# Graph kernel on one Trainium2 core: the node stage moved into the convolution's loop, two node tiles beside every three edge groups

## The reference

```
y0, y1 = x0 @ lin1_w0, x1 @ lin1_w1          # per node, times node_vec1 / 8
w      = silu(edge_scalars @ fc_w1 / sqrt(8)) * 1.679 @ fc_w2 / 8   # per edge
mids   = products of w, y[src] and edge_attr # per edge, 512 wide
agg    = segment_sum(mids, dst) / sqrt(20)   # per node
o      = agg @ lin2 / sqrt(128)              # per node, times node_vec1
x1     = layernorm(x + sin(pi/8) * (x @ sc_w) + cos(pi/8) * o)
xp     = x1 @ lin_w ; a_i, a_j = xp * att    # what the attention layer gathers
```

## Time and profile before

| | |
|---|---|
| median of three runs | 4669.1 us (4668.15 to 4671.51) |
| profiled execution, own time | 4665.0 us |
| its span in the trace | 4663.6 us |
| PE busy | 4158.5 us (89%) |
| DVE busy | 3623.9 us (78%) |
| POOL busy | 3212.8 us (69%) |
| ACT busy | 1445.1 us (31%) |
| convolution's loop | about 81 to 2197 us |
| node stage | about 2197 to 2508 us |
| attention | 2514 us to the end |

### The profile page before, as it was taken

How to read it: one execution, slowest core, us unless ns; L and a number is a source line. 1 busy time by engine, 2 the same in 40 slices (tenths; PEclk the granted TensorE clock), 3 DMA queues, 4 the chain that set the end, 5 groups by cost and what they waited for, 6 DMA issues and landing times. The chain is left out here.

```text
span 4663.6 us, 115274 instructions
## 1 busy us (share of the span) xinstructions
PE 4158.5 (89%) x33992; PEld 2693.8 (58%) x33992; DVE 3623.9 (78%) x10643; ACT 1445.1 (31%) x3213; POOL 3212.8 (69%) x3384
## 2 busy tenths in 40 slices
PE   6988888888888888887997899999988999899997
PEld 5444444444444444443996666777666776666675
DVE  3777777777777777775775888888888888888887
ACT  4111111111111111111553344444444444444444
POOL 3777777777777777775003777777777777777774
PEclk8999999999999999999997888788888788888888
DMA  7444444444444444445774444444444444444443
GB/s 267 133 131 132 131 132 131 132 131 131 131 132 132 131 132 131 132 131 138 281 297 166 122 124 125 123 123 125 122 124 124 124 124 122 125 123 123 125 122 88
DMA packets 375419, 649.80 MB, mean 139 GB/s; under 512 B 130024, under 2 KB 249914, under 8 KB 373548
## 3 DMA queue, kind: packets, MB, share of 16 engines
q0 software_dynamic: 161120, 444.76, 34.6%
q1 hardware_dynamic: 214220, 204.13, 13.5%
HBM read 546.90 MB, written 101.68 MB: 139 GB/s over the span
## 5 line engine op out<-in xcount | busy, mean ns | idle before, releaser
L1995 POOL DMA_INDIRECT ord_xg<-xpa_rows,ord_meta x1666 | 1596.5, 958 | 510.9 <-issue 472.9
L869 POOL DMA_INDIRECT sub_xg<-y_rows,sub_meta x1668 | 1595.3, 956 | 510.5 <-issue 462.8
L2063 PE MATMUL ord_a<-ord_xg,ord_sel 128*128 128x264 f32 x3332 | 1144.5, 478 | 115.4 <-DVE ord_xg L2426 115.2
L919 PE MATMUL sub_a<-sub_mids,sub_sel 128*32 128x128 f32 (+1 forms) x13344 | 998.5, 305 | 228.8 <-DVE sub_mids L1081 221.2
L2063 PEld LDWEIGHTS ord_a<-ord_xg,ord_sel 128*128 128x128 f32 x3332 | 723.0, 238 | 254.3 <-DVE ord_xg L2426 122.9
L1081 DVE TENSOR_TENSOR sub_mids<-sub_w,sub_xg 128x384 f32<-128x384 f32 x1668 | 844.2, 548 | 0.0
L919 PEld LDWEIGHTS sub_a<-sub_mids,sub_sel 128*32 128x32 f32 x13344 | 438.1, 109 | 692.3 <-DVE sub_mids L1081 586.3
L1076 DVE TENSOR_TENSOR sub_mids<-sub_w,sub_xg 128x256 f32<-128x256 f32 x834 | 354.3, 425 | 522.0 <-DMA sub_xg<-y_rows,sub_meta 373.3
L989 ACT ACTIVATE sub_agg_s<-sub_a 128x256 f32<-128x256 f32 x556 | 213.9, 385 | 1618.6 <-PE sub_a L936 1543.3
L899 PE MATMUL sub_w<-sub_fc,sub_ht 64*128 64x256 f32 x3336 | 586.7, 429 | 0.0
L2426 DVE TENSOR_TENSOR ord_xg<-ord_xg,ord_prob 128x1024 f32<-128x1024 f32 x476 | 510.3, 1072 | 0.0
(11 more groups left out here) (183 smaller groups left out, 4153.4 us busy)
## 6 DMA issues: line engine op xcount, KB each, us to landing
sub_sum_rows<-sub_agg_s SPq DMA_DIRECT2D x556, 64.0 KB
mid_rows<-sub_sum_rows SPq DMA_DIRECT2D x14, 2240.0 KB, 8.7
sub_xg<-y_rows,sub_meta POOLq DMA_INDIRECT x1668
ord_xg<-xpa_rows,ord_meta POOLq DMA_INDIRECT x1666
ord_x_rows<-x_rows SPq DMA_DIRECT2D x119, 128.0 KB, 2.2
out_dram<-ord_res SPq DMA_DIRECT2D x119, 128.0 KB
xpa_rows<-mid_proj SPq DMA_DIRECT2D x14, 924.0 KB, 5.3
lin_xt<-in_x_t_dram SPq DMA_DIRECT2D x14, 896.0 KB, 9.9
```

The source lines that it names most:

```text
L869: nc.gpsimd.indirect_dma_start(xg[:, b, k], None, y, bass.IndirectOffsetOnAxis(ids[:, b, 0, k:k + 1], 0))\
L919: mm = nc.tensor.matmul(a[ROWS * m:ROWS * (m + 1), 0:w].rearrange("p (q f) -> p q f", f=MUL), sel[:, b, k, m], of, start=(j == 0), stop=False,
L1995: nc.gpsimd.indirect_dma_start(xg[:, b, k], None, xpa, bass.IndirectOffsetOnAxis(ids[:, b, k:k + 1], 0))\
L2063: mm = nc.tensor.matmul(psum_a[b % 2][:, 0:WIDE], sel[:, b, k], xg[:, b, k], start=(k == 0), stop=(k == TILES - 1 and not has(i, b, -1)), ...
```

## The change

`end_convolution` is no longer called on this path. A pair of node tiles (256 nodes) is worked on beside the three groups of a turn, in turns 1 to 45 (`with_pair`, `LOOP_PAIRS`). Pair i - 1 belongs to turn i. The four pairs that are left (`TAIL_PAIRS`) follow the loop in a short pipeline of their own. A pair may be done in turn i because all groups before turn i have then been summed and the nodes are sorted; the fit test of the inputs got a row for that (`late`). PE's node steps use the PSUM bank of `hidden` (`psum_h`) in turns with it, and stand ahead of the `weigh` of their pair of tiles. `hidden` moves from ahead of `add_up` of u = 1 and 3 to behind `weigh` of u = 0 and 1. Six more DMAs stand in SP's list in a turn. The diff, cut to its core:

```diff
+TURN_SUBS = SUB_TURN * GROUP_SUBS
+SUB_TURNS = math.ceil(SUB_GROUPS / SUB_TURN)
+NODE_PAIR = 2 * P
+NODE_PAIRS = NODES_PAD // NODE_PAIR
+LOOP_PAIRS = SUB_TURNS - 2
+TAIL_PAIRS = NODE_PAIRS - LOOP_PAIRS
...
+                def load_x(n, buf, past):
+
+                    if past is not None:
+                        wait_alone(sp, z_done, past)
+                        wait_alone(sp, pre_done, past)
+                    sp.dma_start(node_xt[:, buf].rearrange("p c j n -> p c (j n)"),
+                                 pair_xt_dram[:, :, bass.ds(n * NODE_PAIR, NODE_PAIR)]).then_inc(x_in[buf], 16)
+                    sp.dma_start(node_x[:, buf].rearrange("p j f -> p (j f)"), pair_rows(io["x"], n))\
+                        .then_inc(x_in[buf], 16)
...
+                def load_sums(n, buf, subs, past):
+
+                    if past is not None:
+                        wait_alone(sp, turned, 2 * past)
+                    wait_alone(sp, stored, stored_subs(subs))
+                    sp.dma_start(node_rows[:, buf].rearrange("p j q f -> p (j q f)"), pair_rows(sums, n))\
+                        .then_inc(sums_in[buf], 16)
...
+                def store_pair(n, buf):
+
+                    wait_alone(sp, out_done, n + 1)
+                    sp.dma_start(pair_rows(x1, n), out[:, buf].rearrange("p j f -> p (j f)")).then_inc(x1_out[buf], 16)
+                    wait_alone(sp, p_copied, 2 * n + 2)
+                    sp.dma_start(pair_rows(xpa, n), proj[:, buf].rearrange("p j f -> p (j f)"))\
+                        .then_inc(proj_out[buf], 16)
+                    sp.dma_start(pair_rows(att, n), proj_a[:, buf].rearrange("p j f -> p (j f)"))\
+                        .then_inc(proj_out[buf], 16)
...
@@ -841,12 +921,30 @@
                             load(g, b, i)
                         if is_pair(i, 0) and b == 0:
                             weights()
+                        if b == SUB_TURN - 1 and with_pair(i):
+                            load_x(i - 1, 0, None if is_pair(i, 1) else i - 1)
+                        if b == 0 and is_pair(i, SUB_TURNS - 1):
+                            for n, buf, times, _, _ in tail:
+                                load_x(n, buf, LOOP_PAIRS if times > 1 else None)
                         if has(i, b, -SUB_TURN):
                             store(g - SUB_TURN, b)
-                    if type(i) is int and i > 0:
+                    if with_pair(i):
+                        load_sums(i - 1, 0, TURN_SUBS * i, None if is_pair(i, 1) else i - 1)
+                        if not is_pair(i, 1):
+                            store_pair(i - 2, 0)
...
+                    if is_pair(i, SUB_TURNS - 1):
+                        for n, buf, _, _, _ in tail[0:-1]:
+                            load_sums(n, buf, TURN_SUBS * i, None)
+                        store_pair(LOOP_PAIRS - 1, 0)
                         for g in range(SUB_TURN * i, SUB_GROUPS):
                             store(g, g % SUB_TURN)
-                        sp.wait_ge(stored, stored_subs(SUBS))
+                        load_sums(tail[-1][0], tail[-1][1], SUBS, LOOP_PAIRS)
...
+                def bank_of_hidden(i, b, u, g):
+
+                    if (b, u) == (0, 4):
+                        pe.wait_ge(silu_done, 2 * g + 4)
+                        turn_sums(i - 1, 0, 0, psum_h)
+                    if (b, u) == (0, 5):
+                        pe.wait_ge(turned_copied, 2 * i - 1)
+                        turn_sums(i - 1, 1, 0, psum_h)
+                    if (b, u) == (1, 2):
+                        pe.wait_ge(silu_done, 2 * g + 4)
+                        add_self(i - 1, 0, i, psum_h)
+                    if (b, u) == (2, 2):
+                        pe.wait_ge(silu_done, 2 * g + 4)
+                        turn_normed(i - 1, 0, psum_h)
+                    if (b, u) == (2, 3):
+                        project(i - 1, 0, psum_h)
+                    if (b, u) == (2, 4):
+                        pe.wait_ge(p_copied, 2 * i - 1)
+                        project(i - 1, 1, psum_h)
...
-                            if u in (1, 3) and more:
-                                hidden(g + 1, after, after_i, u // 2, False)
                             for k in (2 * u, 2 * u + 1):
                                 add_up(g, b, i, k)
                                 if k % RUN == RUN - 1:
                                     hand_on(g, b, i, k // RUN)
+                            if with_pair(i):
+                                bank_of_hidden(i, b, u, g)
                             if u + 2 < PAIRS:
                                 weigh(g, b, u + 2, False)
                             elif more:
                                 weigh(g + 1, after, u + 2 - PAIRS, False)
+                            if u < 2 and more:
+                                if u == 0:
+                                    free_hidden(i, b)
+                                hidden(g + 1, after, after_i, u, False)
...
-                        for s in range(GROUP_SUBS):
-                            if s in (1, 2) and has(i, b, 1):
-                                silu(g + 1, (b + 1) % SUB_TURN, s - 1, not has(i, b, 1 - SUB_TURN))
-                            copy_out(g, b, i, s)
+                        more, early = has(i, b, 1), not has(i, b, 1 - SUB_TURN)
+                        if more:
+                            silu(g + 1, (b + 1) % SUB_TURN, 0, early)
+                        copy_out(g, b, i, 0)
+                        if more:
+                            silu(g + 1, (b + 1) % SUB_TURN, 1, early)
+                        copy_out(g, b, i, 1)
+                        if b == 2 and with_pair(i):
+                            take_normed(i - 1, psum_h, first)
+                            take_projected(i - 1, 0, 0, past, psum_h)
+                        copy_out(g, b, i, 2)
+                        if b == 0 and with_pair(i):
+                            take_sums(i - 1, 0, psum_h, first)
+                        if b == 2 and with_pair(i):
+                            take_projected(i - 1, 1, 0, past, psum_h)
+                        copy_out(g, b, i, 3)
+                        if b == 0 and with_pair(i):
+                            take_sums(i - 1, 1, psum_h, first)
+                        if b == 1 and with_pair(i):
+                            root(i - 1)
...
+                def fold(n, j, buf, times, first):
+
+                    dve.wait_ge(sums_in[buf], 16 * times)
+                    if not first:
+                        dve.wait_ge(turned, 2 * n + j - 1)
+                    f, rows = fold_rows[:, j], node_rows[:, buf, j]
+                    nc.vector.tensor_reduce(f[:, 0:MUL], rows[:, 1:4, 0:MUL].rearrange("p q f -> p f q"), AX, ALU.add)
+                    nc.vector.tensor_copy(f[:, MUL:].rearrange("p (q f) -> p q f", f=MUL), rows[:, 1:4, MUL:])\
+                        .then_inc(folded, 1)
+
...
+                def with_products(i, b, u):
+
+                    if (b, u) == (0, 4):
+                        fold(i - 1, 0, 0, i, is_pair(i, 1))
+                        fold(i - 1, 1, 0, i, is_pair(i, 1))
+                    if (b, u) == (1, 4):
+                        add_x(i - 1, 0, i, psum_h, is_pair(i, 1))
+                    if (b, u) == (1, 5):
+                        moments(i - 1)
+                    if (b, u) == (2, 1):
+                        normalise(i - 1, 0, None if is_pair(i, 1) else i - 1, is_pair(i, 1))
...
-                convolve_in_order(nc, io, c, y, sub_sums, kept)
-                end_convolution(nc, io, c, sub_sums, x1, xpa, att, 5, kept)
+                convolve_in_order(nc, io, c, y, sub_sums, x1, xpa, att, kept)
```

More of the change, by code:

```diff
@@ new lines, in turn_normed, with project @@
+                def turn_normed(n, buf, bank):
+                    pe.wait_ge(out_done, n + 1)
+                    for j in range(2):
+                        for h in range(2):
+                            mm = nc.tensor.transpose(bank[:, (2 * j + h) * P:(2 * j + h + 1) * P],
+                                                     out[:, buf, j, h * P:(h + 1) * P], c["ident"][:])
+                    mm.then_inc(t_done, 1)
+                def project(n, j, bank):
+                    pe.wait_ge(t_copied, n + 1)
+                    for h in range(2):
+                        mm = nc.tensor.matmul(bank[:, 0:FEAT + 2 * HEADS], out_t[:, j, h], c["w_proj"][:, h],
+                                              start=(h == 0), stop=(h == 1), skip_group_check=True)
+                    mm.then_inc(p_done, 1)
@@ L944, in turn, with free_hidden @@
+                def free_hidden(i, b):
+                    if b == 0 and with_pair(i) and not is_pair(i, 1):
+                        pe.wait_ge(p_copied, 2 * i - 2)
+                    if b == 1 and with_pair(i):
+                        pe.wait_ge(turned_copied, 2 * i)
+                    if b == 2 and with_pair(i):
+                        pe.wait_ge(pre_done, i)
                 def turn(i):
@@ new lines, in add_x @@
```

(48 more changed lines are left out.)

157 lines of the change are left out of this document (144 added, 13 removed).

## The result

The changed kernel takes **4819.8 us** (median of 4 runs, 4812.06 to 4826.46) against 4668.6 us (4667.36 to 4671.51) of the kernel before, measured beside it: ratio 1.0322, interval 1.0304 to 1.034. It is 151 us slower. The forecast was 4718 us, 50 us slower than before. The direction was right and the time lies inside the range given (4550 to 4840 us), but the loss is three times the one forecast. The profiled execution took 4819.5 us with a span of 4818.1.

A forecast was written before the change was run, and what follows sets the result against it. POOL's gathers were taken to set the pace, SP's list nearly as full. Removing 316.7 us and adding a 48 us tail gives 4396; 45 turns growing 7.05 us give 4713, put at 4718 us against the median; range 4550 to 4840.

The forecast's parts named there:

- The saving: Between the loop's last copy and the attention's first DMA: 316.7 us go, except for a tail.
- The late sums: At DVE's fold: sums land 23.1 us after SP's load, so DVE and PE stand still 5 us a turn.
- SP's list alone: SP's DMA list in a turn: 43.95 us as before plus six more DMAs, 50.1 us without contention.
- the 1 to 3 us put on top for delayed landings: SP's queue: the pair's 1.7 MB of transfers delay the landings of stores, 1 to 3 us a turn.
- the 51 to 53 us of that paragraph: Length of a turn by SP's list: 50.1 us plus 1 to 3 us for delayed landings.
- the 52.5 us of the next one: Length of a turn by the fold's wait: 38 - 8.6 + 23.1 us, ends 49.5 and 56.
- PE and DVE in a turn: Their work in the loop with the node steps added: 46.3 to 49 us a turn, 47 taken.
- some 2 us: Of PE's 40.5 us of earlier work a turn, this much was called modelled ends of matmuls.
- costs nothing more: PE's node steps ahead of `weigh` in the loop add no time where DVE still has a pair to multiply.
- from the fold to the end of group 3i + 2 PE needs 38 us: PE's stretch in the loop after the fold: 47 - 9.7 us and some slack.
- rival B: In the loop PE's standstill lowers its clock, 2 to 4 us more a turn, 4804 to 4916 us; chance 0.12.
- The tail: Four pairs left after the loop, up to the attention's first DMA: 48 us, bounds 35 and 60.

The follow-up runs named there:

- experiment 1: Changed kernel without the node stage's arithmetic, its six transfers a pair kept in SP's list; a turn takes 49.5 us.
- Experiment 4: Changed kernel with the fold of the sums two pairs later, transposes and products moved behind it; 4646.6 us, ratio 0.9938 to the kernel before.
- experiment 2: Changed kernel with the node arithmetic kept but no loads of sums or x in the loop after the first pair, and no stores; a turn takes 48.9 us.
- experiments 3 and 8: 3: changed kernel with PE's node step behind `weigh`, 4837.1 us; 8: same, plus fold two pairs later and x loads and stores on ScalarE's queue, 4680.1 us.
- Experiment 5: Changed kernel with twenty useless identity transposes on PE ahead of its wait for the fold, fold still late; 4756.0 us, ratio 1.0194 to the kernel before.
- experiments 11 and 12: A hundred useless PE transposes before the tail's sums: 11 on the twenty-transpose kernel, 4759.8 us; 12 on the steps-later kernel with ScalarE's queue, 4597.3 us.
- experiments 9 and 10: 9: changed kernel with a pair's steps one group later, 4682.3 us; 10: the same with x loads and stores on ScalarE's queue, 4593.0 us.

## Why the prediction was right in direction and wrong in size

**The saving** was right: the stage of 316.7 us is gone and the attention behind it is unchanged.

**The late sums** were right, in their place and nearly in their numbers: 22.8 us from the load to the fold in the mean (23.1), a wait of the fold of 3.8 us a turn (5). **SP's list alone** takes 49.5 us, as added up from the rows (50.1); the 1 to 3 us put on top for delayed landings are not seen in experiment 1, which carries all the transfers. So the 51 to 53 us of that paragraph did not confirm the 52.5 us of the next one, although they looked alike. Experiment 4 shows that this wait makes the change slower than the kernel before; a fold two pairs later turns +3.2% into -0.6%.

**PE and DVE in a turn** were undersized by 1.9 us (47 taken, 48.9 measured) with bounds of 46.3 to 49. The prediction's terms without the "some 2 us" of modelled ends are 46.3 + 0.5 + 0.9 + 1.2 = 48.9; no run shows that these 2 us can be taken off, and in experiment 2 PE is busy 46.9 us of each turn. It reached the total only in part, since the late sums and not this sum set the turn: in the stretch from the fold to the next load it is 0.4 us (29.8 against 29.4). That PE's steps stand ahead of `weigh` "costs nothing more" held as well: DVE's longest wait for weight products is 3.9 us once in each turn, in experiment 2 just as in the changed kernel, and the opposite order gained nothing in experiments 3 and 8.

**The step that failed** is "from the fold to the end of group 3i + 2 PE needs 38 us", because it took PE's work at the clock of the kernel before. With the standstill it is done partly at half rate: 31.5 instead of 29.8 us from the fold to the load in the mean, where the prediction had 29.4. The three turns of the changed kernel in which the clock stayed at 1.00 took 51.9 to 52.0 us, and 52.5 was forecast. I had this as rival B with a chance of 0.12, and had kept it apart from the forecast, although the forecast itself holds the standstill that brings it about. Experiment 5 gets 64 us of it back. My 2 to 4 us a turn for it were somewhat high: it is 1.7 us in the mean and 2.1 in the 25 turns of the lowest clock. The turns with a pair took 54.4 us, at the lower end of B's 54.5 to 57, and 4820 us lies within B's 4804 to 4916: what happened is the forecast's late sums together with B. The Trainium skill, page "TensorE: Matmul & The Clock Gate", section "HAM oscillation — how this bites in real kernels", describes a loop that waits for a DMA in each round and starts each time at the lower clock. The trace agrees in 41 of 44 turns, with 0.50 to 0.74 over 6.6 us, but not in three at 1.00; and in the turn shown the clock is still 1.00 when PE starts again, and falls while it works (0.88 from 1516.50 to 1520.00 us, then 0.57 to 1523.00).

**The 91 us of the loop.** The 45 turns with a pair took 54.4 us where 52.5 was forecast, which is 86 us, and 45.4 us before where the forecast had 45.45, which is 3. The rest, 2 us, is a start 4 us later, a first turn 0.6 us longer and a last group 3 us shorter.

**The tail** took 61.7 us against 48, outside its bounds of 35 to 60. The first fold came 14.1 us after the last copy (9): three more stores of the group before the last stood in SP's list, and its load of the sums came only at 2614.98. From there to the last copy of the tail 44.6 us passed (33), and the step to the attention was shorter, 3.05 us against 5.9. For the 11.6 us in the middle the windows show half clock in the tail's first pair and full clock from the third on, and PE mostly at work:

```profile
2604.80:2619.00 14.20, 0.00 (x0) 0.00 (x0) 0.12 (x1) 0.38 (x1) 0.00 (x0) 0.61 0.29 93
2619.00:2628.00 9.00, 7.43 (x32) 6.76 (x32) 1.18 (x5) 2.48 (x3) 0.00 (x0) 0.50 0.58 187
...
2640.00:2650.00 10.00, 8.34 (x56) 7.09 (x55) 5.84 (x23) 3.31 (x11) 0.00 (x0) 1.00 0.16 57
```

The same eight products, in the first pair and in the third:

```profile
2622.28 2.08 PE L1057 MATMUL sub_w<-lin,sub_rows_t 128*128 128x128 f32 x8 [0.69 <-ACT sub_rows_t L1191]
...
2643.60 1.13 PE L1057 MATMUL sub_w<-lin,sub_rows_t 128*128 128x128 f32 x8 [0.88 <-issue]
```

From its first transpose to the end of its products the first pair takes 8.1 us (2619.66 to 2627.77), the second 7.4 (2630.90 to 2638.26, at 0.61 to 0.78) and the third 4.8 (2641.68 to 2646.52). That makes an estimate of 6 us of the 11.6 for the clock, read from the trace and not tested, as experiments 11 and 12 did not keep the clock up; the rest stays open.

## What to carry to other kernels

A stage that is tucked into a loop arrives with its transfers, and these join a queue: add up that queue's list for one turn, follow when the data of the moved step land, and put the step behind that moment. A forecast that contains a standstill of TensorE in each turn must price the work behind it at the lower clock, not keep that as another case. When steps move, their loads and stores have to move too, or go to a queue with room (experiments 9 and 10).

## What was not expected of the hardware

- Twenty useless transposes a turn made the kernel 64 us faster (4820 to 4756): the granted clock behind the fold was 1.00 in 35 of 44 turns, against 3 of 44 without them, while DVE waited as long as before for its sums (3.7 us in the mean in both).
- The same kind of wait did not lower the clock alike in each turn: behind folds that had waited 3.00 and 3.59 us the next 6.6 us ran at 1.00 and at 0.50.
- In experiment 11 some 11 us of full work (a hundred transposes) did not carry the clock over the 5 idle us behind them: 1.00 in one window, 0.53 in the one after.
- ScalarE's queue took five DMA issues a turn at no visible loss in experiment 10: T stayed within 0.3 us of the arithmetic alone (49.2 against 48.9).
- Loads of 640 KB landed in 5.2 us (median of 49) beside gathers, where I had put 4.2 between the 2.2 and 8.7 us of smaller and larger ones.
